# Tables folded through to q, k and v, 1/sigma turned by TensorE, a re-slotted step, and the output's last sum by ScalarE and GpSimd, in a one-layer language-model tower

## What is computed

```python
nesting, segments = syntax_info(token_ids)              # 16 and 8 values
h = concat([pos_table, nest_table[nesting], seg_table[segments]], -1) @ W
x = (h - mean(h)) / sqrt(var(h) + 1e-5)
q, k, v = split_heads(x @ qkv_w.T + qkv_b)               # 8 heads of 16
h = h + (softmax(q @ k.T / 4) @ v) @ out_w.T + out_b
y = layernorm(h)
w = gate(y)           # softmax over 4 experts less a threshold, clipped, normalised
h = h + sum_e w[e] * ((relu(y @ fc1[e].T) @ loA[e]) @ loB[e]) @ fc2[e].T
```

## Time and profile before

| | |
|---|---|
| median of 3 runs | 1199.8 us (1199.28 to 1201.93) |
| profiled execution | 1200.39 us, span 1198.6 us |
| TensorE products | 1112.8 us busy, 93% of the span |
| VectorE | 910.2 us, 76% |
| ScalarE | 823.0 us, 69% |
| GpSimd | 592.8 us, 49% |
| maxima (L882) | 1024, 669.9 us, mean 680 ns |
| exponentials (L507) | 1024, 576.8 us, mean 598 ns |
| q and k products (L662) | 128 records, 69.8 us |
| value products (L635) | 2048 records, 274.0 us |

### The profile page before, as it was taken

The page is one execution under the profiler, slowest core; times in us unless marked ns, Lnnn a source line. Parts: engine busy times, 40 slices in busy tenths (PEclk is TensorE's granted clock), DMA queues, the critical chain, the costliest instruction groups (busy, mean ns, idle before and its releaser), DMA issues.

```text
span 1198.6 us, 20409 instructions
## 1 busy us (share of the span) xinstructions
PE 1112.8 (93%) x6392; PEld 455.6 (38%) x6392; DVE 910.2 (76%) x2370; ACT 823.0 (69%) x1602; POOL 592.8 (49%) x588
## 2 busy tenths in 40 slices
PE   2579999999999999999999999999999999999975
PEld 1223334444344434434344444443443444433322
DVE  6288888877888788777888887778888877788322
ACT  0217777777777777777777777777777777777841
POOL 2644555456544555565445655654455555622231
PEclk9669999999999999999999999999999999999997
DMA  3534534545454345454444455444444454441111
GB/s 84 130 81 97 123 88 113 120 110 123 103 120 105 102 106 119 116 120 105 117 107 102 102 120 125 111 107 114 112 102 100 118 127 109 109 102 44 54 56 36
DMA packets 88377, 123.98 MB, mean 103 GB/s; under 512 B 17469, under 2 KB 69054, under 8 KB 82054
## 3 DMA queue, kind: packets, MB, share of 16 engines
q1 hardware_dynamic: 86720, 121.08, 43.0%
q10 hardware_dynamic: 1550, 1.59, 0.5%
HBM read 80.81 MB, written 34.95 MB: 97 GB/s over the span
## 4 chain that ended last, share of the span: by engine, by line
PE 59%; DVE 20%; issue 4%; DMA 1%; POOL 1%; ACT 0%; SPq 0%; POOLq 0%; DVEq 0%
PE pv L635 14%; PE mix L645 12%; PE sc L624 11%; DVE negmax L882 11%; PE mix L697 7%; PE mix L662 4%; PE mix L713 3%; PE mix L702 2%; PE mix L680 2%; PE mix L657 2%; DVE out_sb L961 2%; DVE rden L901 1%; PE mix L673 1%; DVE onehot L861 1%; DVE mres L892 1%
## 5 line engine op out<-in xcount | busy, mean ns | idle before, releaser
L882 DVE TENSOR_REDUCE negmax<-mix 128x1 f32<-128x512 f32 x1024 | 669.9, 680 | 173.3 <-PE mix L645 166.2
L507 ACT ACTIVATE probs<-sc 128x512 f32<-128x512 f32 x1024 | 576.8, 598 | 183.8 <-PE sc L624 179.4
L624 PE MATMUL sc<-qstk,kstk 120*128 120x512 bf16 x1024 | 366.8, 381 | 0.8 <-ACT probs L507 0.6
L645 PE MATMUL mix<-kstk,qstk 96*128 96x512 bf16 x1024 | 357.2, 392 | 10.0 <-DVE negmax L882 4.8
L635 PE MATMUL pv<-probs,vals 128*32 128x512 f32 x2048 | 274.0, 601 | 0.0
L645 PEld LDWEIGHTS mix<-kstk,qstk 96*128 96x128 bf16 x1024 | 99.7, 98 | 347.2 <-DVE negmax L882 198.1
L460 POOL TENSOR_TENSOR ctxh<-ctx_sb,rdenb 128x512 f32<-128x512 f32 x64 | 81.3, 1271 | 258.7 <-DMA rdenb<-rden_dram 258.2
L624 PEld LDWEIGHTS sc<-qstk,kstk 120*128 120x128 bf16 x1024 | 99.5, 98 | 106.1 <-issue 36.6
L697 PE MATMUL mix<-xn2T,fc1T_sb 128*128 128x512 f32 x256 | 131.9, 599 | 0.0
L416 POOL TENSOR_TENSOR hb_sb<-h_sb,obias 128x512 f32<-128x512 f32 x32 | 40.7, 1273 | 121.6 <-DVE h L907 121.6
L565 ACT ACTIVATE hid<-mix 128x512 f32<-128x512 f32 x128 | 76.8, 600 | 24.2 <-PE mix L697 24.2
(11 more groups left out here) (116 smaller groups left out, 1067.8 us busy)
## 6 DMA issues: line engine op xcount, KB each, us to landing
stack_dram<-pieces SPq DMA_DIRECT2D x192, 128.0 KB
rdenb<-rden_dram SPq DMA_DIRECT2D x64, 256.0 KB
qstk<-stack_dram SPq DMA_DIRECT2D x32, 384.0 KB, 6.6
kstk<-stack_dram SPq DMA_DIRECT2D x32, 384.0 KB, 8.7
qstk<-stack_dram SPq DMA_DIRECT2D x32, 256.0 KB, 6.9
kstk<-stack_dram SPq DMA_DIRECT2D x32, 256.0 KB, 9.3
wrow<-w_dram SPq DMA_DIRECT2D x32, 256.0 KB
out<-out_sb SPq DMA_DIRECT2D x32, 256.0 KB, 2.7
```

The costliest lines, as they stand in the source:

```text
L507: act.activation(probs[:, c % 8, i % 2], sc[:, i % RING], ACT.Exp).then_inc(s_exp, 1)
L624: pe.matmul(sc[:, i % RING, :], kstk[0:KROWS, u, h, j * P:(j + 1) * P], qstk[0:KROWS, u, h, :], start=True, stop=True).then_inc(s_score, 1)
L645: pe.matmul(max_bank(m), qstk[0:STK, u, h, j * P:(j + 1) * P], kstk[0:STK, u, h, :], start=True, stop=True).then_inc(s_mxmm, 1)
L882: dve.tensor_reduce(negmax[:, m // NT, m % NT:m % NT + 1], max_bank(m), AX.X, ALU.max, negate=True).then_inc(s_max, 1)
```

## The change

q, k and v are no longer computed from the normalised rows. Since h is a sum of table rows, its centred product with the weights is too: at the start the kernel folds table and positions through (I - 1/128) and the three weight matrices. `table` becomes four tables (embedding, q, k, v), and q, k and v come from the one-hot matrix in bf16. The positions' part (`posQK`, `posV`) is added in float32, and the result is multiplied by 1/sigma. The products by slot are now 0 project, 1 embed (t+4), 2 fc1_3 (t-3), 3 low, 4 none, 5 xn2T, 6 out, 7 gates, 8 turn_gates, 9 q (t+4), 10 fc1_0, 11 mT, 12 fc1_1, 13 k (t+4), 14 fc1_2, 15 v (t+4).

- VectorE adds the positions to q in slot 10 and to k in slot 14 (`add_qk`); `add_pos` and the first statistics move from slots 11 to 13 to slots 2 to 5; the one-hot matrix is made in slot 15 for t+5, which adds a step -5.
- GpSimd multiplies q and k by 1/sigma (`scale`), adds the positions to v and multiplies it into `vals` (`value`); `norm` goes.
- 1/sigma lies by token along the partitions, so for q and k TensorE turns it (`turn_rstd`, in mT's bank), ScalarE copies it out (`copy_rT`), and SP stores it and loads it as a row for all partitions (`store_rstd`, `load_rstd`).
- The final sum: ScalarE copies the experts' output from PSUM (`copy_experts`), GpSimd adds h2 (`finish`, before on VectorE).
- The copy of the head rows into kstk moves from VectorE to ScalarE, ahead of its first step, and the output's store moves behind the load of 1/sigma in SP's list.

```diff
 PRODUCTS = [
-    ("project", -2), ("xnT", 3), ("q", 3), ("low", -3), ("k", 3), ("xn2T", -2), ("out", -3), ("gates", -2),
-    ("turn_gates", -2), ("v", 3), ("fc1_0", -2), ("embed", 4), ("mT", 1), ("fc1_1", -2), ("fc1_2", -2), ("fc1_3", -2),
+    ("project", -2), ("embed", 4), ("fc1_3", -3), ("low", -3), ("none", None), ("xn2T", -2), ("out", -3), ("gates", -2),
+    ("turn_gates", -2), ("q", 4), ("fc1_0", -2), ("mT", 1), ("fc1_1", -2), ("k", 4), ("fc1_2", -2), ("v", 4),
 ]
-BESIDE = {3: 3, 7: 7, 11: 12}
+BESIDE = (3, 7, 11)
 ACT_WORK = [
-    (1, 1, "xnT", 3, 0), (2, 1, "qk", 3, 0), (4, 0, "ctx", -1, 1), (4, 2, "qk", 3, 1), (5, 2, "xn2T", -2, 0),
-    (8, 0, "gates", -2, 0), (9, 0, "gate_exp", -2, 0), (9, 1, "v", 3, 0), (10, 1, "relu", -2, 0),
-    (12, 0, "mT", 1, 0), (12, 0, "ctx", 0, 0), (12, 1, "wT", -2, 0), (13, 1, "relu", -2, 1), (14, 1, "relu", -2, 2),
-    (15, 1, "relu", -2, 3),
+    (1, 2, "qk", 3, 0), (2, 2, "relu", -3, 3), (3, 1, "qk", 3, 1), (4, 0, "ctx", -1, 1), (5, 2, "xn2T", -2, 0),
+    (6, 1, "experts", -3, 0),
+    (8, 0, "gates", -2, 0), (9, 0, "gate_exp", -2, 0), (10, 1, "relu", -2, 0),
+    (12, 0, "mT", 1, 0), (12, 0, "ctx", 0, 0), (12, 1, "wT", -2, 0), (12, 1, "rT", 4, 0), (13, 0, "relu", -2, 1),
+    (14, 1, "relu", -2, 2), (15, 2, "v", 4, 0),
 ]
 DVE_WORK = [
     (0, 1, "add_attention", -2, 0), (1, 0, "stats2", -2, 0), (1, 1, "stats2", -2, 1), (2, 0, "moments2", -2, 0),
-    (4, 0, "weigh", -3, 0), (6, 1, "finish", -3, 0), (7, 1, "invert_den", -1, 0), (8, 1, "gate", -2, 0),
-    (9, 1, "gate", -2, 1), (9, 2, "hot", 4, 0), (10, 0, "gate", -2, 2), (10, 0, "gate", -2, 3),
-    (11, 1, "add_pos", 4, 0), (12, 0, "stats1", 4, 0), (12, 1, "stats1", 4, 1), (13, 0, "moments1", 4, 0),
+    (2, 1, "add_pos", 4, 0), (3, 0, "stats1", 4, 0), (3, 1, "stats1", 4, 1), (4, 0, "weigh", -3, 0),
+    (5, 0, "moments1", 4, 0), (7, 1, "invert_den", -1, 0),
+    (8, 1, "gate", -2, 0), (9, 1, "gate", -2, 1), (10, 0, "gate", -2, 2), (10, 0, "gate", -2, 3),
+    (10, 1, "add_qk", 4, 0), (14, 0, "add_qk", 4, 1), (15, 2, "hot", 5, 0),
 ]
 POOL_WORK = [
-    ("add_bias", 3, 0), ("rstd2", -2, 0), ("norm2", -2, 0), ("second", 3, 0), ("residual", 3, 0), ("third", 3, 0),
-    ("second", 3, 1), ("residual", 3, 1), ("third", 3, 1), ("normalise", -1, 0), ("rstd1", 4, 0), ("norm", 4, 0),
+    ("scale", 3, 0), ("add_bias", 3, 0), ("scale", 3, 1), ("rstd2", -2, 0), ("norm2", -2, 0),
+    ("second", 3, 0), ("residual", 3, 0), ("third", 3, 0), ("rstd1", 4, 0),
+    ("second", 3, 1), ("residual", 3, 1), ("third", 3, 1), ("normalise", -1, 0), ("v", 3, 0), ("finish", -3, 0),
 ]
 SP_WORK = [
-    ("ids", 4, 0), ("piece", 3, (0, 0)), ("den_out", -1, 1), ("piece", 3, (0, 1)), ("piece", 3, (0, 2)),
-    ("den_in", -1, 0), ("piece", 3, (1, 0)), ("piece", 3, (1, 1)), ("out", -3, 0), ("piece", 3, (1, 2)),
-    ("rden_out", -1, 0), ("rden_in", -1, 0), ("den_out", 0, 0), ("max_in", 1, 0), ("weights_out", -2, 0),
-    ("weights_in", -2, 0), ("stack", 3, 0), ("stack", 3, 1),
+    ("ids", 5, 0), ("piece", 3, (0, 0)), ("piece", 3, (1, 0)), ("den_out", -1, 1), ("piece", 3, (0, 1)), ("den_in", -1, 0),
+    ("piece", 3, (0, 2)), ("piece", 3, (1, 1)), ("rden_out", -1, 0), ("piece", 3, (1, 2)),
+    ("rden_in", -1, 0), ("den_out", 0, 0), ("max_in", 1, 0), ("weights_out", -2, 0), ("rstd_out", 4, 0),
+    ("weights_in", -2, 0), ("rstd_in", 4, 0), ("out", -3, 0), ("stack", 3, 0), ("stack", 3, 1),
 ]
...
+            def load_rstd(b):
+                upto(sp, s_scaled, b - 1, 2)
+                upto(sp, s_rstdout, b, 16)
+                sp.dma_start(rstdb[:], rstd_dram.rearrange("j p -> (j p)").partition_broadcast(P)).then_inc(s_rstdin, 16)
...
+            def scale(b, side):
+                upto(pool, s_rstdin, b, 16)
+                upto(pool, s_raw, b, 2, side + 1)
+                pool.tensor_tensor(qk32[:, side, :], qk32[:, side, :], rstdb[:], ALU.mult).then_inc(s_scaled, 1)
...
+            def finish(b):
+                upto(pool, s_experts, b)
+                pool.tensor_tensor(out_sb[:], out_sb[:], h2[:, b % H2], ALU.add).then_inc(s_out, 1)
...
             pool.wait_ge(s_setcp, 4)
             pool.wait_ge(s_const, 3)
+            pool.wait_ge(s_pos, 3)
...
+            for side in range(2):
+                act.wait_ge(s_fold2mm, 2 + side)
+                act.copy(posQK[:, side, :], sc[:, 1 + side]).then_inc(s_pos, 1)
+            act.wait_ge(s_fold2mm, 4)
+            act.copy(posV[:], pv[:].rearrange("p (j n) -> p j n", j=NT)).then_inc(s_pos, 1)
+            act.copy(kstk[STK:KROWS, 0, :, :],
+                     const_sb[STK:KROWS, 4:4 + NH].unsqueeze(2).broadcast_to([3 * NH, NH, S])).then_inc(s_const, 1)
             act.wait_ge(s_const, 4)
...
             def copy_qk(b, side):
-                upto(act, (s_qmm, s_kmm)[side], b)
-                upto(act, s_pc1, b - 1, 2, side + 1)
-                upto(act, s_res0, b - 1, 2, side + 1)
-                act.activation(qk32[:, side, :], aux("qk"[side], 1), ACT.Identity,
-                               bias=(qb_sb[:], qkb_sb[:, 1:2])[side], scale=(QSCALE, 1.0)[side]).then_inc(s_qk32, 1)
+                upto(act, s_scaled, b, 2, side + 1)
+                act.activation(qk32[:, side, :], qk32[:, side, :], ACT.Identity,
+                               bias=(qb_sb[:], qkb_sb[:, 1:2])[side]).then_inc(s_qk32, 1)
...
+            def add_qk(b, side):
+                upto(dve, (s_qmm, s_kmm)[side], b)
+                if b == 0:
+                    dve.wait_ge(s_pos, 2)
+                upto(dve, s_pc1, b - 1, 2, side + 1)
+                upto(dve, s_res0, b - 1, 2, side + 1)
+                dve.tensor_tensor(qk32[:, side, :], aux("qk"[side], 1), posQK[:, side, :], ALU.add).then_inc(s_raw, 1)
```

238 lines of the change are left out of this document (161 added, 77 removed).

## The result

| | before | changed |
|---|---|---|
| median of the runs | 1200.55 us | 1278.57 us (1274.77 to 1281.15) |
| span of the profiled execution | 1198.6 us | 1277.0 us |
| changed / before, 95% interval | | 1.0647 (1.0617 to 1.0677) |

The change costs 78 us. The forecast was 1203 us with a range of 1175 to 1224: wrong, and outside its range. The starts of the attention addition (L1031 now) in VectorE's timeline answer to the earlier trace rows; the four rows are those of steps 2, 14, 15 and 28. Columns: start, length, engine, line, operation, shapes, and what ended the idle time before it.

What follows compares the result with a forecast made beforehand. It took TensorE's own work plus waits for VectorE to bound the kernel. Full steps -3.9, start +13.7, light steps -4.6, steps 28 and 29 -3.3, last output +1.2 made +3.1: 1203 us, range 1175 to 1224.

Steps and rivals of the forecast that it cites:

- the three waits: Once-a-step waits of TensorE in slots 2, 10 and 12 for read-outs: A, B and C.
- B: Slot 10: TensorE's second row tile waits for VectorE's addition of positions to q, 1.75 us a step.
- A: Slot 2: TensorE's second row tile waits for VectorE's addition to the embedding, 0.85 to 0.9 us a step.
- C: Slot 12: TensorE's second row tile waits for ScalarE's copy of 1/sigma, 0.3 us a step.
- TensorE's own work: TensorE's time in a full step without waits: from 33.1 to 30.7 us, 2.4 less.
- Rival 1: Faster: VectorE less late, so B's or A's wait goes; 1172 us (1164 to 1182), chance 0.20.
- Cost nothing, cover about 3 us: SP's waits for 1/sigma's trip: row in 3.3 us, landing just before slot 0, scalings needed 3 us later.
- Rival 2: Slower: 1/sigma lands 3 us late, delaying ScalarE's cut of q and the exponentials; 1230 to 1255 us, chance 0.08.
- The ports: VectorE's cast of the maxima slowed by GpSimd's chain through shared SBUF ports: 0.1 us a step, up to 0.8.
- rival 3: Slower: GpSimd's chain ends just later and the cast pays 0.8 us, not 0.1; 18 us, 1222 us, chance 0.10.
- The start: Up to the first score product: stacks issued 16.4 us late, 2.7 regained; net +13.7 us, bounds +9 and +18.
- The light steps: Steps 0 and 1, without the layer's second half: from 27.9 to 25.6 us each, -4.6 together.

Runs made afterwards that it cites:

- c3: Changed kernel with 1/sigma's round trip through memory issued earlier and two copies of the pieces' buffer in memory, nothing left out: 1213.68 us.
- e1: c3 with q's addition before slot 10's first maximum, the gates' last parts behind it, and GpSimd's normalising held until the gates' last product: 1180.77 us.
- e4: e2 with GpSimd's list re-ordered at its head and the embedding's addition ahead of slot 2's first maximum: 1162.27 us.
- a3: Changed kernel with 1/sigma's round trip made for the first sequence only, later factors wrong: 1223.52 us.
- c2: Changed kernel with 1/sigma turned in slot 7 and its round trip issued earlier, nothing left out: 1222.41 us.
- b1: Kernel before the change, with only the first piece of k moved ahead of the store of the sums in SyncE's list: 1234.15 us.
- a1: Changed kernel with two copies of the pieces' buffer in memory, used in turn: 1257.87 us.
- a2: Changed kernel with the first piece of k moved back behind the load of the sums in SyncE's list: 1259.43 us.
- c1: Changed kernel with the edits of a1 and a3 together, plus a wait ahead of the stack loads: 1215.24 us.
- e2: e1 with ScalarE's copy of the head rows and its three loads moved to step t = -3, behind slot 9: 1174.47 us.
- f2: e4 with GpSimd's work on the values held until the cut of the maxima is done: 1158.40 us.

## Why the prediction was wrong

**TensorE's work and the three waits: the right places, and a sum that is right partly by luck.** With the faults out (c3) a full step is 33.93 against the 33.98 of the sum. The reader was named rightly for each wait. But B, forecast at 1.75, is 1.56, A, at 0.9, is 0.68 (in the changed kernel, with 1/sigma late, 1.1 on average), C, at 0.3, is 0.18 in the changed kernel and gone in c3, whose 1/sigma lies in another bank, and q's product in c3 waits in two steps only: 2.35 us without work a step against 3.25. TensorE's own work, put at 30.7 us, is 31.6 in c3 by its busy time in the 26 steps (820.9 us). By the same measure it was 33.5 before, so the change takes 1.9 us a step off it, not 2.4. Two errors of 0.9 us cancel. (The 26 steps of before are 34.08 us long and not 34.13, another 1.4 us in the forecast's -3.9.) Rival 1 (faster, if B and A went) was the right mechanism for the wrong kernel: e1 to e4 take them away and land at 1181 to 1162 us.

**"Cost nothing, cover about 3 us": the step that failed.** It holds two errors. The way in of 1/sigma's row was taken at 3.3 us "nearer to the broadcast's row", and the text says a few sentences on that the output's store and the stack loads stand behind it, without asking what they do to its landing. Measured 5.8. And the sum lets SyncE issue the store as soon as ScalarE's copy is done; in the full steps it was issued 1.26 us (median) behind the copy's end, after the turned maxima and the weights. From the copy's start to the scaling it took 10.0 us (596.97 to 606.97) where the sum had 5.9, so it landed 3.3 us into slot 0 and not at its edge. Rival 2 set its point at 3 us late and its time 27 to 52 us above the forecast; a3 and c2 take 55 and 56 us off. It got a chance of 0.08, against "no hop in the rows took that long". The rows of hops, though, had no stack loads behind them. Its path was not the one that counted either: it had the exponentials behind ScalarE's cut of q, and ScalarE did wait 46.4 us for the scaling, but TensorE waited only 1.0 us for exponentials. The loss came by the cut of the maxima (q's product) and by the embedding's addition (A). How much of it is held-up casts and how much the later start of the cut was not taken apart.

The other error is in SyncE's list. I followed the new entries and not the old one that moved: the first piece of k, from behind the load of the sums to ahead of their store. In before its wait for the k stack was always met by then. b1 shows 33 us for this move alone in the kernel before, a1 and a2 19 to 21 in the changed one, and 8 to 9 are left once the trip is out of the way (a3 to c1, c2 to c3). So of the 65 us between the changed kernel and c3 the trip is the larger part.

**The ports: the right mechanism, the wrong size, and not independent.** 0.1 us a step was forecast, with rival 3 at 18 us. The cut rose by 20.1 us over the whole run (45.6 against 25.5). The text says that GpSimd's chain ends at T + 2.6 and the cast starts at T + 2.33; with the scaling 3.3 us late the chain could only end later. With 1/sigma in time, in c3, the first cast takes 0.29 us on average, the forecast's 0.1 above 0.19. Rivals 2 and 3 were given separate chances although the one brings the other about; together they reach 1248 to 1273 us, beyond the range and near the result. A second place, the gates' last product, was in no rival: 11.4 us in the changed kernel against 5.6 in before.

**The start: +13.7 forecast, +17.2 measured** (+16.2 in c3). The stacks are issued at 55.92 us, forecast 56.0. The 2.7 us that were to come back behind the landing did not: from the first row tile (68.34) to the first score it is 39.7 us, as before. The cut meets GpSimd there too (a cast of 1.00 and a subtraction of 1.20 us from 93.85 on), which is 1.8 us against 0.8 in before; the rest was not traced. The head rows on ScalarE were costed at 3.9 and their loads at 2.42: e2 measures both together at 6.3.

**The light steps: -4.6 forecast, +10.8 measured**, +0.9 in c3. "A and B nearly vanish" was wrong: in c3 A is 1.33 and 0.95 us in these two steps and B 0.95 in each, 4.2 us together, where before had neither. The cut meets GpSimd there as well in all variants (step 0 in c3: 1.12 and 1.18 us); in f2, which takes most of that away, with A and B re-ordered, the stretch is 53.8 us against the forecast's 52.6. (By the prediction's own terms, 57.2 less 1.7, a light step of before is 27.8 and not 27.9.) Why steps 0 and 1 lost another 10 us in the changed kernel was not tried by itself; the waits for the sums there (2.3 us at 155.76) point to SyncE's list.

**What was to show it.** "GpSimd not waiting for rstdb beyond the start of slot 0" and "casts above 0.19 us" were the right places to look, and both went against the forecast; so did "waits of ScalarE for the scaling", which it named as the sign upwards (46.4 us, 33 times). The first score product, "near 105", came at 108.08.
